# Local attention's mask: added by VectorE while it takes the row maximum, instead of by a TensorE product

## The reference

```python
def local_attention(q, k, v):
    ...
    bk, bv = (look_around(bk), look_around(bv))
    ...
    sim = jnp.einsum('bhwid,bhwjd->bhwij', bq, bk)
    i = bt[:, :, None]
    j = btk[:, None, :]
    mask = (i < j) | (i > j + WINDOW) | (j == -1)
    sim = jnp.where(mask, -jnp.finfo(sim.dtype).max, sim)
    attn = jax.nn.softmax(sim, axis=-1)
    out = jnp.einsum('bhwij,bhwjd->bhwid', attn, bv)
```

## Time and profile before

| | |
|---|---|
| time of three runs | 3232.84, 3233.68 (median), 3268.52 us |
| the profiled execution | 3231.55 us, its span 3229.8 us, 1.75 us around it |
| granted TensorE clock, mean | 0.944 of full speed |
| TensorE busy | 2873.4 us of the span, 89% |
| VectorE busy | 1565.0 us, 48% |
| ScalarE busy | 1166.9 us, 36% |
| GpSimd busy | 1066.9 us, 33% |

### The profile page before, as it was taken

One profiled execution on the slowest core, in us unless ns is written; L12 is line 12 of the kernel. 1 busy time (PEld: TensorE's weight loads), 2 busy tenths in 40 slices (PEclk: granted clock), 3 DMA queues, 4 the chain that ended last, 5 costly groups with the idle time before them and its releaser, 6 DMA issues. The chain is left out here.

```text
span 3229.8 us, 41719 instructions
## 1 busy us (share of the span) xinstructions
PE 2873.4 (89%) x15902; PEld 1893.9 (59%) x15902; DVE 1565.0 (48%) x2994; ACT 1166.9 (36%) x2240; POOL 1066.9 (33%) x770
## 2 busy tenths in 40 slices
PE   6999899999989899898999899999988759999990
PEld 3565656556565655545554555555554349989990
DVE  5645456565545556475656565666654410000002
ACT  3444343434343344343444444444432212222221
POOL 4423233342323234252535344443432311111112
PEclk8999999999999999899999999999998679999995
DMA  3000000000001011001010101010101069998874
GB/s 126 10 20 17 24 26 24 14 24 20 17 23 48 21 50 45 14 4 46 4 46 4 47 4 46 4 46 4 40 4 40 2 230 351 349 339 328 324 296 159
DMA packets 86048, 261.69 MB, mean 81 GB/s; under 512 B 10940, under 2 KB 50188, under 8 KB 67164
## 3 DMA queue, kind: packets, MB, share of 16 engines
q1 hardware_dynamic: 79372, 241.26, 20.6%
q0 software_dynamic: 6480, 17.77, 1.4%
HBM read 210.69 MB, written 44.12 MB: 79 GB/s over the span
## 5 line engine op out<-in xcount | busy, mean ns | idle before, releaser
L1171 POOL TENSOR_TENSOR s_qk<-s_qk,s_rrec 128x1024 f32<-128x1024 f32 (+1 forms) x128 | 215.1, 1681 | 761.4 <-DVE s_rrec L1317 761.3
L547 PE MATMUL s_pA<-s_w_wqkv,s_curT 128*128 128x512 f32 x768 | 372.3, 624 | 5.8 <-ACT s_curT L932 3.9
L960 ACT ACTIVATE s_qk<-s_pA,s_mx 128x256 f32<-128x256 f32 (+1 forms) x512 | 221.5, 448 | 420.2 <-DVE s_mx L1313 420.1
L1843 PEld LDWEIGHTS m_ph<-m_xT,m_w 128*128 128x128 f32 x2272 | 267.4, 194 | 5.4 <-issue 1.8
L1843 PE MATMUL m_ph<-m_xT,m_w 128*128 128x128 f32 x2272 | 268.0, 277 | 1.2 <-DVE m_xT L1913 1.2
L1913 DVE COPY m_xT<-m_px 128x256 f32<-128x256 f32 x71 | 30.1, 424 | 476.3 <-PE m_px L1832 476.3
L1857 PE MATMUL m_py<-m_w,m_hT 128*128 128x256 f32 x1136 | 258.1, 381 | 0.0
L547 PEld LDWEIGHTS s_pA<-s_w_wqkv,s_curT 128*128 128x128 f32 x768 | 146.9, 198 | 183.0 <-issue 169.8
L1406 DVE TENSOR_SCALAR s_pairs<-s_pD 128x1024 f32<-128x1024 f32 (+1 forms) x192 | 193.7, 1038 | 105.6 <-PE s_pD L693 67.9
L693 PE MATMUL s_pD<-s_mixer 32*128 32x512 f32 (+3 forms) x1024 | 201.5, 511 | 47.3 <-DVE s_pairs L1406 38.0
L1857 PEld LDWEIGHTS m_py<-m_w,m_hT 128*128 128x128 f32 x1136 | 211.4, 191 | 26.1
(11 more groups left out here) (222 smaller groups left out, 5104.6 us busy)
## 6 DMA issues: line engine op xcount, KB each, us to landing
m_w<-in_m_w SPq DMA_DIRECT2D x142, 1024.0 KB, 5.7
m_xin<-rows_s SPq DMA_DIRECT2D x71, 129.0 KB
m_acc<-acc_s SPq DMA_DIRECT2D x16, 512.0 KB, 5.1
s_cur<-in_x SPq DMA_DIRECT2D x8, 512.0 KB, 3.4
xn_s<-s_cur SPq DMA_DIRECT2D x8, 512.0 KB, 2.6
s_s_tm<-xn_s SPq DMA_DIRECT2D x8, 512.0 KB, 3.2
cur_s<-s_cur SPq DMA_DIRECT2D x8, 512.0 KB, 2.6
s_s<-s_s_tm SPq DMA_DIRECT2D x8, 512.0 KB, 2.6
```

Of the source, the lines that this page charges most:

```text
L547: last = nc.tensor.matmul(out, lhs(c), rhs(c), start=(c == 0), stop=(c == n - 1))
L960: last = nc.scalar.activation(prob[u % 3][:, i * 256 + lo:(i + 1) * 256], ps[:, i * 256 + lo:(i + 1) * 256], ACT.Exp, bias=mx[:, u, i:i + ...
L1171: nc.gpsimd.tensor_tensor(pi, pi, rrec[:, u, :].unsqueeze(2).broadcast_to((P, 4, 256 - lo)), ALU.mult).then_inc(p_rdy, 1)
L1843: last = nc.tensor.matmul(ph[u % 2][:, f * P:(f + 1) * P], w1[:, u % NW, c * F + f * P:c * F + (f + 1) * P], xT[:, u % 2, c * P:(c + 1) * ...
```

## The change

The mask is no longer a product. It stands in SBUF as a 128 x 256 fp32 tile (`maskw`), and `local_max` becomes four VectorE instructions, one a head: each adds the mask to the head's scores, changes the sign, writes the result to SBUF (`prob`), and gives the minimum of it, which is the negated maximum. The exponential then works on SBUF in place with scale -1. The scores leave PSUM with the fourth of these instructions, counted by a new semaphore `outS`; `bank_ring` now returns for each job two counts to wait for, one for jobs that ACT empties and one for jobs that DVE empties. The wait for the transposes of unit u - 3, which use the same probability buffer, moves from ACT to DVE. `local_reciprocal` waits for a new semaphore `exp_rdy` in the same place.

```diff
+    colsA, waitA, doneA = bank_ring(ring_a, ("S",))
+    colsD, waitD, doneD = bank_ring(ring_d)
...
-        maskw = sb("maskw", [P, 2, P], BF16)
+        maskw = sb("maskw", [P, 2 * P])
...
-                if waitA[k] > 0:
-                    pe.wait_ge(outA, waitA[k])
+                if waitA[k][0] > 0:
+                    pe.wait_ge(outA, waitA[k][0])
+                if waitA[k][1] > 0:
+                    pe.wait_ge(outS, waitA[k][1])
...
-                for bank in range(2):
-                    nc.tensor.matmul(ps[:, bank * 512:(bank + 1) * 512].rearrange("p (h k q) -> p h k q", h=2, k=2)[:, :, lo:2, :],
-                                     identb[:], maskw[:, lo:2, :].unsqueeze(1).broadcast_to((P, 2, 2 - lo, P)), start=True, stop=False)
...
-                                            qkT[r, 4 + h // 2, (t - 1 + lo) * P:(t + 1) * P], start=False, stop=(i >= 2))
+                                            qkT[r, 4 + h // 2, (t - 1 + lo) * P:(t + 1) * P], start=True, stop=True)
...
             def local_exp(b, u):
-                act.wait_ge(mx_rdy, 2 * NT * b + u + 1)
-                if u >= 3:
-                    act.wait_ge(mmA, AJ["PT", b, u - 3] + 1)
-                else:
-                    act.wait_ge(mmA, AJ["qkT", b, u] + 1)
-                ps = takeA("S", b, u)
+                act.wait_ge(outS, doneA["S", b, u])
                 lo = 0 if u // 2 else P
                 for i in range(4):
-                    last = nc.scalar.activation(prob[u % 3][:, i * 256 + lo:(i + 1) * 256], ps[:, i * 256 + lo:(i + 1) * 256], ACT.Exp,
-                                                bias=mx[:, u, i:i + 1], accum_out=rsum[:, u, i:i + 1])
-                last.then_inc(outA, 1)
+                    pi = prob[u % 3][:, i * 256 + lo:(i + 1) * 256]
+                    last = nc.scalar.activation(pi, pi, ACT.Exp, scale=-1.0, bias=mx[:, u, i:i + 1], accum_out=rsum[:, u, i:i + 1])
+                last.then_inc(exp_rdy, 1)
...
             def local_max(b, u):
                 dve.wait_ge(mmA, AJ["S", b, u] + 1)
+                if u >= 3:
+                    dve.wait_ge(mmA, AJ["PT", b, u - 3] + 1)
                 lo = 0 if u // 2 else P
-                nc.vector.tensor_reduce(mx[:, u, :], heads(pA[:, colsA[AJ["S", b, u]]], 4)[:, :, lo:256], AX.X, ALU.max, negate=True).then_inc(mx_rdy, 1)
+                ps = pA[:, colsA[AJ["S", b, u]]]
+                for i in range(4):
+                    h = slice(i * 256 + lo, (i + 1) * 256)
+                    last = nc.vector.tensor_tensor_reduce(out=prob[u % 3][:, h], in0=ps[:, h], in1=maskw[:, lo:256], scale=-1.0, scalar=3e38,
+                                                          op0=ALU.add, op1=ALU.min, accum_out=mx[:, u, i:i + 1])
+                last.then_inc(outS, 1)
```

## The result

The changed kernel takes 3195.2 us, the median of four runs (3189.4 to 3200.6), and the kernel before took 3233.3 us in four runs on the same chip. The ratio is 0.987 with an interval of 0.983 to 0.991: 1.3% faster, where 1.6% was forecast.

What follows compares the result with a forecast made beforehand. The bound was TensorE's work plus, in the u loops, a score unit's round trip. 31 + 5 + 3 + 9 = 48, rounded 50 us off 3231.55, plus 2 for the median: 3183 us, range 3142 to 3232.

Steps and rivals of the forecast that it cites:

- the seven retention stages 0 to 6: Stages modelled on stage 2: each gains 4.4 us by unit 4 and nothing after, 31 us in all.
- stage -1: Stage with only local attention: units 4.05 us apart instead of 5.0, some 2 us at units 2 and 3; 5 us.
- the seven latent stages: Stages modelled on stage 9: the DVE and POOL chain leaves a gain of 1.3 us each, 9 us in all.
- D: Time of a unit's four new VectorE instructions: 1.8 us taken, 0.45 us each, between bounds of 1.4 and 2.6 us.
- the prediction's own slope: Each 0.1 us of D moves a retention stage 0.4 us, a latent one 0.25 to 0.3, together about 5 us.
- rival 3: TensorE's clock: one more half-clock stretch a stage returns 22 us, 3205 us; chance 0.15 together with Rival 5.
- L595 and the waits for L960: Sign on TensorE: both gone, replaced by waits before L609 and, before units 6 and 7, for ACT's copy L971.
- Retention loop 4 to 5 us shorter: Sign in stage 2's u loop: 4 to 5 us shorter than 63.4 us.
- Latent loop 1 to 2 us shorter: Sign in stage 9's u loop: only 1 to 2 us shorter than 82.2 us.
- Rival 1: Only the banks' round trip matters: latent stages gain 4.4 us each, or D is lower; 3151 us, chance 0.25.
- Rivals 2 and 4: VectorE: 2, 0.65 us a head, 3223 us, chance 0.10; 4, instructions held up, D 4.8 us, 3334 us, chance 0.05.
- Rival 5: Mask products not really saved, in units 0 to 3 too: 25 us less gain, 3208 us; 0.15 together with rival 3.

Runs made afterwards that it cites:

- e3: The changed kernel with ACT's copy of the transposed probabilities put ahead of the exponentials in its queue: 3181.4 us, ratio 0.984.
- e4: The changed kernel with GpSimd's power for the latent tokens' layer norm put ahead of the scaling of probabilities 2: 3188.9 us, ratio 0.985.
- e1: The kernel before without its mask products, the mask left out of the computation, everything else unchanged: 3242.6 us, ratio 1.001.
- e10: The kernel before without mask products (mask left out) and with dead products in TensorE's waits in latent stages: 3209.7 us, ratio 0.992.
- e6: The changed kernel with 24 dead products, read by nobody, ahead of TensorE's waits in each latent stage: 3160.0 us, ratio 0.976.
- e7: Control on the changed kernel: the dead-product code with the same order of bank requests and waits, but no dead product: 3192.4 us, ratio 0.987.
- e2: The changed kernel with the mask products back on TensorE; VectorE adds a constant 1e-24 instead, freeing banks as early: 3209.2 us, ratio 0.991.
- e8: The changed kernel with ACT's copy first, GpSimd's power first and 24 dead products a latent stage: 3143.7 us, ratio 0.972.
- e11: The changed kernel with ACT's copy first, GpSimd's power first and 14 dead products a latent stage: 3120.3 us, ratio 0.964.

## Why the prediction was right, and what in it was wrong

The time was right in part by luck: errors of opposite sign nearly cancel. Against the forecast of 48 us, the seven retention stages 0 to 6 gave 36.7 us instead of 31, stage -1 11.3 instead of 5, stage 7 3.5 instead of 3; the seven latent stages lost 11.8 us instead of gaining 9, and what follows them lost 2.6 where nothing was expected. The sum is 37.

**D was too high.** It measured 1.4 to 1.5, not 1.8 us, since the read of the accumulator lies beside the next instruction. By the prediction's own slope, 5 us for each 0.1 us, 1.4 alone gives 3163 us. Retention stages 1 to 4 bear the slope out: forecast 4.4 us each, plus 4 x 0.4 for D, makes 6.0, and stages 1 to 4 gained 5.6. All seven together gained 36.7 where this makes 42.

**Stage -1** gave 11.3 where 5 was forecast. Its spacing was about right, 3.9 us from scores to scores (4.05 forecast, 5.0 before), but scores 3, from which it counts, come at 61.3 us instead of 66.6: units 2 and 3 gave 5.2 us rather than 2, because before they sat behind long waits and at half clock, and scores 4 follow them by 3.0 instead of 6.0 us.

**The latent stages failed in sign.** Each of the seven was to gain 1.3 us, at D = 1.4 some 2.4. Stage 8 gained 6.0, the other six, 9 to 14, lost 3.0 each on average. The step that failed is the one on rival 3, "I expect neither as a rule". The loss isn't one half-clock stretch a stage, as that rival had it: the retention loop of the earlier trace rows stands at 1.00, and most latent ones lose several stretches each. But not all of them do: the u loops of stages 9, 11, 12, 13 and 14 in the changed kernel's windows are

```profile
1417.00:1499.00 82.00, 69.11 (x459) 46.31 (x456) 48.08 (x142) 34.44 (x86) 29.82 (x25) 0.94 0.08 27
...
1755.30:1837.40 82.10, 69.19 (x455) 46.45 (x452) 47.89 (x141) 34.71 (x86) 29.84 (x25) 0.93 0.07 27
1921.00:2009.00 88.00, 77.59 (x460) 51.82 (x459) 48.43 (x141) 36.02 (x87) 29.83 (x25) 0.83 0.07 25
2093.00:2181.00 88.00, 76.71 (x457) 50.50 (x456) 47.93 (x140) 35.33 (x88) 29.83 (x25) 0.86 0.07 25
...
2266.30:2354.30 88.00, 75.36 (x459) 49.74 (x459) 48.32 (x141) 34.46 (x87) 29.84 (x25) 0.86 0.05 19
```

Stages 9 and 11, at 0.94 and 0.93, last 166.0 and 166.3 us, 1.8 and 0.9 less than the 167.8 and 167.2 of before; stages 10 and 12 to 14, at 0.83 to 0.86, last 171.8 to 173.2, some 5 us more. The one pair of loops at an equal clock is stage 9's, 0.94 in both kernels: 84.2 us before, 82.0 after, a little more than the 1 to 2 us forecast for a loop. Stage 11's loop, 0.96 before and 0.93 after, is 0.4 us longer (82.2 to 82.6), and its gain lies ahead of the loop (85.0 to 83.7). The same code, one stage apart, comes out on either side.

The books of stages 9 to 14: TensorE's busy time should have gone from 919.7 to some 897 us by the masks removed (6 x 3.8) and was 928.8, so some 32 us are put down to the clock; idle time rose by 8.7, from 84.2 to 92.9 us, and which wait that is was not followed; 32 + 8.7 - 23 = 17.7, the 17.8 measured. The clock's own rows bear the size out: at 0.96 over 1003.9 us some 40 us of full clock are missing, at 0.92 over 1021.7 us some 82, and TensorE was idle in a part of them.

The gain of the dead work is not a second measurement of it, though it is 31.5 us in these stages (1023.9 to 992.4): it takes the clock to 0.97, above the 0.96 of before, and what that gives back is lessened by what the products cost, as busy time rises by 13.8 us and idle time falls by 45.3. That 3160.0 us lies near the 3163 of the forecast at D = 1.4, and stages 9 to 14 1.9 us each below before, fits the forecast's arithmetic but does not show it.

**The signs to look for.** The four instructions take 1.46 us from first to last instead of 1.7 to 1.9: wrong. L595 and the waits for L960 are gone, and TensorE waits before L610 (L609 before) and before scores for the copy (L969, before L971), as said: right. Retention loop 4 to 5 us shorter: 5.7. Latent loop 1 to 2 us shorter: wrong, 5.7 us longer. "Wrong, if the granted clock of the stream leaves 0.97" is what happened: 0.95 over the stream, 0.92 in stages 9 to 14, where it was 0.96. "Wrong, if latent stages shorten as much as retention ones" is true of stage 8 alone.

**The rivals.** Rival 1's D was right, its latent stages (4.4 us gained each) were not; whether those chains have slack is not settled, as e3 and e4 gain nothing there at a low clock. What it had for it, that TensorE's idle times name the exponential and nothing else, was read wrongly: the earlier trace rows has a wait for `s_zT`, and the kernel before waits for 24.3 us on L1406 before L693 and for 13.1 us on the scaled probabilities before L609. Rivals 2 and 4 fall with D = 1.4. Rival 5 is answered by e1 and e10: the mask products are saved for the greater part (27 of 38 us by stage 9), and it is the clock that takes this back later. Rival 3 named the mechanism, at 22 us in 16 stages where some 32 were lost in six. That a lower clock is what costs the time is shown by e6 against e7; that it fell because TensorE had less to do between its waits is argued, from its fall in e1 and e2 and its rise with dead work in e6, e8, e10 and e11, and which of the waits in a latent loop matters was not tried one by one. Why stages 9 and 11 escape is open. Of e2's 19.4 us, 2.9 are idle time whose chain was not followed.

## What to carry to other kernels

Before work is taken off the engine that bounds a kernel, look at the granted clock of the stretches with idle time in them: less work at a lower clock can take longer, and then the gain is in shorter waits, not in less work. A loss of this kind is told from a longer chain by one pair of kernels, one with dead work ahead of the waits and one with the same code and none. And in the queue of an engine that serves the bound one, it is worth trying the copy that frees or fills its buffers ahead of the long operation: here it gave 0.9 us a retention stage, and in latent stages it showed only together with a second such change.

## What the runs showed of the hardware

- The same code at 0.94 and at 0.83 of the granted clock differs by some 6 us in a stage of 166, and both occur in one execution, in stages next to each other.
- A VectorE instruction with an accumulator output, 256 columns from PSUM and SBUF, starts 0.35 us after the one before it; its second instruction, 0.08 us, runs beside the next one.
- Taking only mask products away from TensorE left the time where it was (1.001), and adding 24 dead products to each latent stage of the changed kernel took 1% off it, with the granted clock of the loop going from 0.83 to 0.98.
- Four exponentials with row sums of 256 columns take 1.98 us from SBUF, 1.81 us from PSUM.
